# A mixed kernel of four transformer layers: 32 moves of the first routed layer issued without the waits between bursts

## The reference

```python
# x = x + _L0_xattn_ref(_layernorm(x), ...)
x = x + _L0_ffn_ref(_layernorm(x), gate_w, fc_w, proj_w)

def _L0_ffn_ref(x, gate_w, fc_w, proj_w):          # E = 8, K = 2, D = 128
    xt = x.reshape(-1, d)                          # 2048 x 128
    gates = jax.nn.softmax(xt @ gate_w, axis=-1)
    top_v, top_i = jax.lax.top_k(gates, K)
    top_v = top_v / jnp.sum(top_v, axis=-1, keepdims=True)
    h = jax.nn.gelu(jnp.einsum('nd,edf->enf', xt, fc_w), approximate=False)   # f = 512
    eo = jnp.einsum('enf,efd->end', h, proj_w)
    sel = jnp.take_along_axis(jnp.swapaxes(eo, 0, 1), top_i[:, :, None], axis=1)
    return jnp.sum(sel * top_v[:, :, None], axis=1).reshape(orig_shape)
```

## Time and profile before

| | before |
|---|---|
| median of 3 runs | 612.33 us (608.09 to 612.35) |
| the profiled execution's own time | 611.6 us |
| its span in the profile | 609.5 us |
| mean granted TensorE clock | 0.932 of full |
| PE, PEld busy | 550.2, 464.0 us |
| DVE, ACT, POOL busy | 408.1, 240.2, 269.1 us |

### The profile page before, as it was taken

One profiled execution on the slowest core, in us unless ns is written; L12 is line 12 of the kernel. 1 busy time (PEld: TensorE's weight loads), 2 busy tenths in 40 slices (PEclk: granted clock), 3 DMA queues, 4 the chain that ended last, 5 costly groups with the idle time before them and its releaser, 6 DMA issues.

```text
span 609.5 us, 12293 instructions
## 1 busy us (share of the span) xinstructions
PE 550.2 (90%) x3808; PEld 464.0 (76%) x3809; DVE 408.1 (67%) x1452; ACT 240.2 (39%) x551; POOL 269.1 (44%) x489
## 2 busy tenths in 40 slices
PE   4999988389999899999999978999999799999992
PEld 3577757289998499888987856766786299999992
DVE  8888873133437885475678868877887765655573
ACT  2555613135554343444442223454551043333330
POOL 3365266656656405930000010444534778874332
PEclk9999868689999889999998989998999599999997
DMA  9999013112243400000000360002200122222234
GB/s 310 379 315 269 2 49 80 57 53 71 70 136 92 120 1 1 2 1 1 1 2 0 103 175 1 2 1 70 70 1 10 57 72 64 69 57 57 78 108 120
DMA packets 48151, 47.64 MB, mean 78 GB/s; under 512 B 6470, under 2 KB 37603, under 8 KB 47942
## 3 DMA queue, kind: packets, MB, share of 16 engines
q1 hardware_dynamic: 43558, 37.68, 21.1%
q0 software_dynamic: 4544, 9.38, 4.7%
HBM read 27.53 MB, written 19.51 MB: 77 GB/s over the span
## 4 chain that ended last, share of the span: by engine, by line
PE 72%; DVE 19%; another core or an unknown queue 3%; issue 3%; ACT 1%; DMA 1%; DVEq 0%; POOL 0%; POOLq 0%; SPq 0%; ACTq 0%
PE bank L2411 16%; PE bank L2422 10%; PE bank L1988 8%; PE bank L2184 4%; PE bank L2229 4%; PE bank L2268 4%; PE bank L2257 2%; PE bank L1977 2%; PE bank L1978 2%; PE bank L1979 2%; PE bank L1868 2%; PE bank L2399 1%; DVE stats L1106 1%; DVE X L1510 1%
## 5 line engine op out<-in xcount | busy, mean ns | idle before, releaser
L2411 PE MATMUL bank<-xT,wcur 128*128 128x128 f32 x936 | 122.1, 282 | 13.4 <-ACT xT L888 7.5
L2411 PEld LDWEIGHTS bank<-xT,wcur 128*128 128x128 f32 x936 | 114.7, 198 | 15.7 <-issue 12.3
L641 POOL TENSOR_SCALAR var_eps<-mv 128x4 f32<-128x4 f32 (+2 forms) x12 | 2.9, 238 | 186.0 <-DVEq L1814 95.7
L698 POOL DMA_INDIRECT yt<-Y,dest_i x62 | 60.9, 983 | 53.6 <-ACT Y L904 29.1
L682 POOL DMA_INDIRECT xw<-XW,slot_i x64 | 63.4, 991 | 30.1 <-issue 15.5
L1440 DVE COPY wcur<-WA 128x512 f32 x78 | 37.7, 485 | 56.9 <-PE bank L2411 34.0
L972 ACT ACTIVATE hT<-bank,b_cols 128x512 f32<-128x512 f32 x64 | 44.0, 688 | 63.3 <-PE bank L1979 62.8
L1988 PE MATMUL bank<-WC,hT 128*128 128x128 f32 x512 | 63.8, 279 | 0.0
L1988 PEld LDWEIGHTS bank<-WC,hT 128*128 128x128 f32 x512 | 61.4, 194 | 1.4
L1584 DVE SCALAR_TENSOR_TENSOR X<-bank,G,X 128x128 f32<-128x128 f32 x128 | 36.0, 344 | 32.3 <-PE bank L1988 27.0
L1455 DVE TENSOR_TENSOR hT<-gb,bank 128x512 f32<-128x512 f32 x39 | 26.8, 688 | 40.2 <-ACT gb L893 37.6
(11 more groups left out here) (404 smaller groups left out, 1191.5 us busy)
## 6 DMA issues: line engine op xcount, KB each, us to landing
xw<-pad_rows SPq DMA_DIRECT2D x34, 260.0 KB, 4.1
xrow<-xw SPq DMA_DIRECT2D x78, 65.0 KB
WA<-in_fc_dram SPq DMA_DIRECT2D x16, 256.0 KB, 4.2
YT<-yt SPq DMA_DIRECT2D x16, 256.0 KB, 3.2
WA<-in_pj_dram SPq DMA_DIRECT2D x8, 256.0 KB, 5.8
WB<-in_fc_dram SPq DMA_DIRECT2D x8, 256.0 KB, 4.7
WB<-in_pj_dram SPq DMA_DIRECT2D x8, 256.0 KB, 6.1
X<-in_x_dram SPq DMA_DIRECT2D x2, 512.0 KB, 4.2
```

The costliest lines, as they stand in the source:

```text
L698: pool.indirect_dma_start(out=yt_dram, out_offset=bass.IndirectOffsetOnAxis(ap=dest_i[:, t:t + 1], axis=0), in_=y_slot(layer, t), in_offse ...
L2411: ins = pe.matmul(dst, wcur[:, s4, at:at + P], xT[s4 % 2][:, :], start=True, stop=True)
```

## The change

The table BURSTS goes. In the first routed layer Pool no longer waits for the landing of the group before ahead of groups 1, 4 and 6. In the second routed layer the one such wait, ahead of group 1, stays. The waits for the group four before stay in both.

```diff
 MOVED = (0, 5, 6, 7, 8, 10, 12, TILES)
-BURSTS = ((1, 4, 6), (1,))
...
                 for group in range(1, last + (layer == 0)):
-                    if group in BURSTS[layer]:
-                        pool.wait_ge(scattered[(group - 1) % RING], landed(layer, group - 1))
+                    if layer and group == 1:
+                        pool.wait_ge(scattered[0], landed(layer, 0))
                     if group >= RING:
                         pool.wait_ge(scattered[group % RING], landed(layer, group - RING))
```

## The result

| | before | after |
|---|---|---|
| median of 9 runs each, taken beside each other | 609.61 us (606.8 to 613.13) | 614.04 us (612.27 to 616.51) |
| ratio after to before, 95% interval | | 1.0065 (1.0035 to 1.0095) |
| the profiled execution's own time, its span | 611.6, 609.5 us | 613.5, 611.4 us |
| first up-matmul of step 0, first down-matmul | 96.5, 101.2 us | 119.9, 124.3 us |
| end of the layer's last down-matmul | 191.7 us | 195.3 us |

The change makes the kernel slower by 0.65%, 4.4 us in the medians. I had forecast 3 us less. The size is inside the band that I called the same; the direction is the other one.

A forecast was written before the change was run, and what follows sets the result against it. TensorE, 90% busy, bounds it, with 18.6 us lost around 102 to 128 us. 5.17 - 0.37 - 1.90 = 2.9, other terms 0: 611.6 less 3 is 608.6, with 0.7 for the median 609.3, said 609; range 598 to 617.5.

The forecast's parts named there:

- the band that I called the same: Whole kernel's time from 606.2 to 618.4 us, about one per cent either side of 612.33; chance 0.60.
- The waits removed, 5.17 us: Pool's scatters, first routed layer: without three landing waits they end 5.17 us earlier, at 115.38 instead of 120.55.
- The loads wait for the steps: SP's loads of xrow: earlier scatters give them almost nothing, since load 9 also waits for DVE's dest_i of step 5.
- the hold: First routed layer, 102 to 128 us: TensorE's reports get through badly while Pool issues scatters in a row; 18.6 us lost.
- The rival in which Pool has nothing to do with it: Reports are held by something with its own clock, the release stays near 126.5: 612 us; chance 0.10.
- How far TensorE gets by the last release: First routed layer's expert steps: two results ready and one TensorE step fewer than before, so 2.9, about 3 us gained.
- the worst end that I gave it: TensorE gets nowhere: release at 116.75, pipeline filled in 5.30 us, step 0's down-matmuls at 122.05, a loss of 2.3 us.
- The price of lost cover at the start: DVE's table read at Pool's gap from 87.44 to 89.16, which goes: at most 6 us later, taken as 0.
- Contention of Pool and DVE, 0: Closer scatters beside DVE's copies of wcur: at most 0.25 us for one scatter, 0 for most, taken as 0.
- the hold starts earlier and lasts longer: Slower rival: unbroken scatters from 74.8 to 115.4 delay reports from 88 us on; typical 615, up to 621 us; chance 0.20.
- the two releases at 109.30 and 120.78: ACT's starts right behind ends of Pool's scatter runs (109.14, 120.55); taken to show some steps pass before 115.38.

The follow-up runs named there:

- p_ind: Kernel before plus 20 indirect Pool transfers of 64 KB in a row behind the first routed layer: 625.06 us against 609.38, one run.
- p_dir44: Kernel before plus 44 plain Pool transfers of 64 KB behind the first routed layer, on another chip: 607.58 us against 606.57, one run.
- e_only1: Kernel before with only the landing wait ahead of group 1 (11th scatter) kept of the three: 612.73 us against 609.38, ratio 1.0045.
- e_only4: Kernel before with only the landing wait ahead of group 4 (17th scatter) kept of the three: 614.96 us against 609.38, ratio 1.0093.
- e_gaps: Changed kernel with Pool memsets in place of the three landing waits: 617.08 us against 616.48 of the kernel before, ratio 0.9986.
- p_ind3: Kernel before plus the same 20 indirect Pool transfers, as control on the chip of p_dir44: 621.71 us against 606.57, one run.
- e_all: Kernel before with landing waits ahead of all groups 1 to 6, three more than before: 617.65 us, ratio 1.0007.

## Why the prediction was wrong

It held where it read rows and failed where it had to say how far TensorE would get.

1. *The waits removed, 5.17 us.* Right. Scatters' end forecast 115.38, measured 115.06; idle times ahead of the three scatters 0.30, 0.47 and 0.30 us. The loads wait for the steps: not put to the test, since no step ran ahead of 119.

2. *What the hold is.* Right, and now shown rather than a coincidence: p_ind makes it at a place of its own, three times on three chips (TensorE 11.9, 11.7 and 13.3 of 20 us), p_dir44 shows that plain transfers don't. The rival in which Pool has nothing to do with it falls. The Trainium skill, "SBUF — State Buffer", section on two separate sides, from which that rival drew, says that TensorE and ScalarE never wait for anyone on the engine side. Of ports that may be so; p_ind shows TensorE brought down to one or two matmuls per 1.40 us by what Pool does. The exception is the fourth chip, on which the same row of Pool makes no hold.

3. *How far TensorE gets by the last release.* This step failed. I took two results ready and one step fewer than before. It got nowhere: the first result came at 125.40. And the worst end that I gave it, down-matmuls at 122.05 with a release 1.37 us behind Pool's last, was too early by 2.3 us: the release came 3.09 us behind (118.15 against 115.06), what it released was an M copy and not yet a step, so that the first transpose followed only at 119.00, and from there the pipeline filled in 5.31 us, as the prediction had it (5.30), to the first down-matmul at 124.31. In p_ind it came 2.7 us behind. Counted back to step 0, before's beat began at 119.8, so the term measured is 4.5 us lost where 2.9 gained stood in the sum. The layer's end shows 3.6 of it, since before lost another 0.9 on the way: its down-matmuls of steps 5 and 6 stand 2.81 us apart (129.27 and 132.08), not 1.90.

4. *The price of lost cover at the start, taken as 0.* Wrong, and with the late M copies this is the cause of 3. I looked for the price in the table and in slot_i only: they are late by 1.8 and 3.3 us, which alone would have cost little, as I said. What I missed were ACT's three M copies between 84 and 118 us. They belong to the attention's preparations, not to the experts, but they stand in ACT's order ahead of the first xT, so the hold on them keeps out the whole layer. In before they start at 90.68, 92.38 and 94.88, between the two breaks at 87 and 96 us: the break at 87 had left only a row of six scatters beside them. The change makes this one row of 32. e_only1 (break at 87 kept: last M copy 2.8 us behind its matmul, first up-matmul 98.7, layer's end 191.3) and e_only4 (break at 96 kept: 20.2 us behind, 115.9, 194.1) tell which break did it, and e_gaps (1.1 us behind, 97.9, 191.2) that a break of memsets does as well.

5. *Contention of Pool and DVE, 0.* Right: the scatters shown take 0.95 to 0.98 us.

The rival that came true is the one on the slower side, *the hold starts earlier and lasts longer*. I gave it 0.20, a typical time of 615 and much of the mechanism that the trace shows: the unbroken run meets the reports from 88 us on, TensorE comes to the release with nothing done, the table is late, the release comes later. It had no M copies in it, and that 615 stands so close to the measured 614 is in part luck. The forecast had the same two facts and rated them otherwise: the sentence on the two releases at 109.30 and 120.78 ("so some steps will pass") rests on a layer that had already begun before the hold closed. Here a hold that met a running pipeline let it limp; one that closed ahead of its first step let nothing pass.

Part of the distance is the baseline: the prediction stood on a median of 612.33, the nine runs beside the result gave 609.61. The effect was forecast as -3.0 and measured as +4.4 us.

## What stays open

Why the hold is there on three of the chips of the experiments (before 606.57 to 616.58 us) and not on a fourth (587.45). What holds the engines back inside is open too. The slow beat (1.40 us in p_ind, 0.70 us in p_ind3), the dependence on the pace and the release some microseconds behind Pool's last transfer would fit a queue that the engines share and that indirect transfers 1.27 us apart fill faster than it empties. That is a guess, which no run tests. The Trainium skill, "NOTIFIC — the notification-queue block", section on the three overflow behaviours, tells of one such queue, that of the records, whose internal pipeline holds back the engines rather than lose a record. No run here shows whether that is what is at work: all executions, the timed ones too, came with their span recorded, so whether the hold is there without records isn't known. Nor was the change run on the chip without the hold. I would expect nothing of it there, since the steps keep their beat through the scatters, but that wasn't tried. Open too is why the second routed layer takes 110 to 121 us in different profiles, and with it why e_only1 is 0.45% slower although its first routed layer ends in time.

## What to carry to other kernels

A wait that looks like pure loss on one engine can be the gap through which the others are served: before it is taken out, look not only at who waits for its end but at what other engines get done during it, among them instructions of an earlier stage that stand in order ahead of the loop. When reports come late without a sender, put the suspected work alone into a quiet stretch, in two kinds and at two paces; two runs there told more than six variants of the schedule. And gains ahead of a bound that moves with them (here Pool's row of transfers, which grows with each result that is ready early) come back as a wait later: all four variants with breaks or pauses at 87 us end the layer between 190.5 and 191.3, before at 191.7.

## What the runs showed of the hardware

Indirect transfers of Pool, 128 rows of 512 or 520 bytes, one every 1.27 us, hold back the other compute engines on three of four chips: a report of TensorE late by up to 24.9 us (the matmul over at 93.25, the copy that needs it at 118.15), VectorE waiting 1.5 us for its own instruction before, and in the probes TensorE down to one or two matmuls per 1.40 us or one per 0.70 us. One every 1.52 us does it hardly in a quiet stretch (18.5 of 20 us busy, one run), but ACT still waits 5.3 and 5.9 us for a report when such a pace follows a denser row (e_all, at 128.3 and 134.8); one every 1.95 us costs TensorE nothing in that stretch (20.0 of 20, one run). Forty-four plain transfers of Pool, one every 0.53 us, don't at all. On the fourth chip the same program has no hold and is 19 to 29 us faster, so a comparison of this kernel across chips says more on the hold than on any edit.
